# A dilation over 121 taps: chains of half-height relus in PSUM with one matmul for each step, twelve pairs added by DMA, and two pairs clamped by GpSimd

## The reference, cut to what matters

```python
v = _gn(x)
pad = jnp.pad(v, ..., constant_values=-1e30)          # 5 rows and columns on each side
for idx in range(121):
    di, dj = idx // 11, idx % 11
    acc = jnp.maximum(acc, pad[:, :, di:di+256, dj:dj+256] - kflat[:, idx])
x = x + acc
x = x + _L1_conv_ref(_gn(x), ...)                     # convolution, batch norm, gelu, bilinear resampling
```

## Time and profile before

| | |
|---|---|
| Time, median of 3 runs | 11728.51 us (11725.23 to 11729.66) |
| Span of the profiled execution | 11726.8 us |
| Dilation, first join to last join (63 chunks) | 367.3 to 9764.3 us |
| Convolution stage | about 9790 to 10700 us |
| Resampling stage | about 10720 us to the end |
| Busy share of the span | PE 89%, DVE 96%, ACT 78%, POOL 85% |

### The profile page before, as it was taken

The page is one execution under the profiler, slowest core; times in us unless marked ns, Lnnn a source line. Parts: engine busy times, 40 slices in busy tenths (PEclk is TensorE's granted clock), DMA queues, the critical chain, the costliest instruction groups (busy, mean ns, idle before and its releaser), DMA issues. The chain is left out here.

```text
span 11726.8 us, 92131 instructions
## 1 busy us (share of the span) xinstructions
PE 10455.5 (89%) x23180; PEld 4353.8 (37%) x23180; DVE 11256.4 (96%) x7096; ACT 9189.6 (78%) x5145; POOL 10018.7 (85%) x3019
## 2 busy tenths in 40 slices
PE   2999999999999999999999999999999997886665
PEld 1333333333333333333333333333333333332222
DVE  8999999999999999999999999999999998998999
ACT  2888888888888888888888888888888886776666
POOL 2999999999999999999999999999999996666777
PEclk9999999999999999999999999999999998998888
DMA  7555555555555555555555555555555553343555
GB/s 280 105 108 105 107 104 106 106 105 100 105 103 105 103 104 103 106 108 108 105 107 108 106 106 106 106 108 105 106 105 107 106 103 128 151 167 157 213 214 213
DMA packets 352237, 1435.57 MB, mean 122 GB/s; under 512 B 18896, under 2 KB 125520, under 8 KB 289616
## 3 DMA queue, kind: packets, MB, share of 16 engines
q0 software_dynamic: 183440, 762.23, 35.9%
q1 hardware_dynamic: 168256, 667.25, 15.3%
HBM read 465.90 MB, written 201.33 MB: 57 GB/s over the span
## 5 line engine op out<-in xcount | busy, mean ns | idle before, releaser
L502 POOL TENSOR_TENSOR m_pool<-r_pool,u 128x2048 f32<-128x2048 f32 x1792 | 7708.4, 4369 | 864.9 <-DVE acc_a L675 556.3
L531 PE MATMUL m_pe<-u,mats 128*128 128x512 f32 x10240 | 5375.2, 606 | 508.0 <-DVE acc_b L657 398.9
L533 PE MATMUL m_pe<-r_pe,mats 128*128 128x512 f32 x10240 | 5273.8, 596 | 0.0
L675 DVE SCALAR_TENSOR_TENSOR acc_a<-m_pool,kt,acc_a 128x2048 f32<-128x2048 f32 x1728 | 4059.9, 2349 | 54.5 <-POOL m_pool L502 41.0
L657 DVE SCALAR_TENSOR_TENSOR acc_b<-m_pe,kt,acc_b 128x1024 f32<-128x1024 f32 x2560 | 3246.0, 1278 | 103.2 <-PE m_pe L533 100.5
L531 PEld LDWEIGHTS m_pe<-u,mats 128*128 128x128 f32 x10240 | 1837.4, 191 | 3285.4 <-issue 1856.8
L533 PEld LDWEIGHTS m_pe<-r_pe,mats 128*128 128x128 f32 x10240 | 1948.4, 190 | 2510.3 <-issue 2510.3
L675 DVE SCALAR_TENSOR_TENSOR acc_a<-u,kt,acc_a 128x2048 f32<-128x2048 f32 x896 | 2103.8, 2348 | 4.5
L621 ACT ACTIVATE r_pool<-dx,gap_l 128x2048 f32<-128x2048 f32 x896 | 1778.6, 1993 | 329.7 <-POOL m_pool L502 326.2
L621 ACT ACTIVATE r_pe<-dx,gap_l 128x2048 f32<-128x2048 f32 x832 | 1659.1, 1994 | 364.2 <-PE m_pe L533 349.9
L592 ACT ACTIVATE t<-dx,gap_r 128x2048 f32<-128x2048 f32 x640 | 1284.7, 2007 | 10.4
(11 more groups left out here) (139 smaller groups left out, 5595.1 us busy)
## 6 DMA issues: line engine op xcount, KB each, us to landing
t<-dx POOLq DMA_DIRECT2D x640, 1059.0 KB, 8.4
u<-x_dram SPq DMA_DIRECT2D x28, 3328.0 KB, 28.7
xw<-x_scratch SPq DMA_DIRECT2D x64, 1152.0 KB, 6.9
hw<-h_scratch SPq DMA_DIRECT2D x66, 1024.0 KB, 8.9
x<-xc POOLq DMA_DIRECT2D x65, 1024.0 KB, 8.0
xt<-x_dram SPq DMA_DIRECT2D x32, 2048.0 KB, 14.4
xc<-x_dram SPq DMA_DIRECT2D x64, 1024.0 KB, 4.7
x_scratch<-x SPq DMA_DIRECT2D x64, 1024.0 KB, 9.6
```

Source lines behind the costliest of these rows:

```text
L502: nc.gpsimd.tensor_tensor(m_pool[slot(s, k, j, NPOOL)][:], r_pool[slot(s, k, j, NPOOL)][:], u[s][:, k * CR + di:k * CR + di + CR, base:bas ...
L531: nc.tensor.matmul(dst, ident, u[s][:, top:top + 2, base:base + W], start=True, stop=False)
L533: last = nc.tensor.matmul(dst, ident, r_pe[slot(s, k, j, NPE)][:, row:row + 2, :], start=False, stop=True)
L675: nc.vector.scalar_tensor_tensor(out=acc_a[:], in0=src, scalar=kt[:, col(di, base):col(di, base) + 1], in1=acc_a[:], op0=ALU.subtract, op1 ...
```

## The change

The 121 taps are divided anew. Per chunk:

- Six row sides become chains (`CHAINS`): in rows di 0 to 2 the columns 0 to 4, in rows 3 to 5 the columns 10 to 5. A chain is folded from the outside in, in PSUM, separately for the two halves of 4 rows (`chain[0]`, `chain[1]`, two banks each): ScalarE's relu (128x1024) reads the chain's banks and writes them back, TensorE adds the next slice of `dx` (with the identity or the negated identity) with one matmul for each bank and `start=False`, and in the last step adds `u`. A left chain has 4 steps, a right one 5: 27 steps, on 2 halves.
- 12 pairs have their relu written to one of three `t` buffers, `u` is added there by DMA (`add_u`), and VectorE reads `t`.
- 24 pairs go over GpSimd. 22 get ScalarE's relu as before. Two (`CLAMPED`) get none: GpSimd clamps a slice of `dx` with `tensor_scalar` into `m_pool` and then adds or subtracts it. `m_pool` has three buffers in place of two.
- 16 single taps, one of which starts `acc_b`.
- The order of each engine is a string of letters (a digit is a chain step or merge of that half; r relu for GpSimd, x relu for a DMA pair, b `start_b`, u sum, n normalise; m, y, s merges of `m_pool`, `t`, `u`; t add, c clamp, i DMA issue, d piece of `dx`, a `add_x`).

```diff
+CHAINS = ((0, "left"), (1, "left"), (2, "left"), (3, "right"), (4, "right"), (5, "right"))
+NPOOL, NDMA = 24, 12
+CLAMPED = (6, 18)
+ACT_ORDER = "x0r10r1x01r01bxr01r01u0rr10xn10r01u01xrn10r1r0nx10x1r01nr01r01xr01r01x01r01r01xr001x01x01r01r1r"
+PE_ORDER = "010101100101010100110101010101010101010101010010101101"
+DVE_ORDER = "smm10ssmmyssm0m1ymymssm0m1ysssmymym01msmmymys0m1ssymmmysm01ymym"
+POOL_ORDER = "ttiadtititdctttitdttitiditttittdicttittidittt"
...
-    NPOOL, NPE, NTRIPLE = 28, 20, 10
...
+    RP, MP, TP = 2, 3, 3
...
+    chain_steps = []
+    for ch, (di, side) in enumerate(CHAINS):
+        bases = range(1, 5) if side == "left" else range(9, 4, -1)
+        chain_steps += [(ch, step, base) for step, base in enumerate(bases)]
...
+                def add_u(c, s, k, j):
+                    di, base, outer = dma_pairs[j]
+                    pool.wait_ge(t_ready, c * NDMA + (j + 1))
+                    passed(pool, pool_turns)
...
+                def clamp(c, s, k, i):
...
+                    pool.wait_ge(a_done, a_free(c, "m", j, NPOOL, MP))
+                    passed(pool, pool_turns)
+                    nc.gpsimd.tensor_scalar(m_pool[j % MP][:], dx[s][:, k * CR + di:k * CR + di + CR, lo:lo + W],
+                                            floor, FAR if right else -FAR, first, second).then_inc(clamp_ready, 1)
+                def pair(c, s, k, j):
...
+                    pool.wait_ge(r_pool_ready, c * NRELU + (relu_no[j] + 1))
+                    pool.wait_ge(a_done, a_free(c, "m", j, NPOOL, MP))
+                    nc.gpsimd.tensor_tensor(m, r_pool[relu_no[j] % RP][:], rows, ALU.add).then_inc(m_pool_ready, 1)
...
-                                    for q in range(2):
-                                        row = (half * 2 + q) * 2
-                                        dst = m_pe[half][:, 2 * q:2 * q + 2, :]
-                                        top = k * CR + di + row
-                                        nc.tensor.matmul(dst, ident, u[s][:, top:top + 2, base:base + W],
-                                                         start=True, stop=False)
-                                        last = nc.tensor.matmul(dst, ident, r_pe[slot(s, k, j, NPE)][:, row:row + 2, :],
-                                                                start=False, stop=True)
...
+                def add_step(c, s, k, h, i):
...
+                    pe.wait_ge(chain_relu[h], c * NSTEP + (i + 1))
...
+                    for r in range(0, HR, 2):
+                        top = k * CR + di + h * HR + r
+                        added = nc.tensor.matmul(chain[h][:, r:r + 2, :], weight, src[:, top:top + 2, dj:dj + W],
+                                                 start=False, stop=True, skip_group_check=True)
+                    added.then_inc(chain_added[h], 1)
...
+                def chain_step(c, s, k, h, i):
...
+                    if step == 0:
...
+                        act.wait_ge(chain_taken[h], at(c, NCHAIN, ch))
+                    else:
+                        act.wait_ge(chain_added[h], c * NSTEP + i)
+                    gap = gap_r if right else gap_l
+                    nc.scalar.activation(chain[h][:], src, ACT.Relu, bias=gap[:, col(di, base):col(di, base) + 1],
+                                         scale=scale).then_inc(chain_relu[h], 1)
...
+                                elif kind == "r":
+                                    behind = relu_pairs[j - RP] - (NPOOL if j < RP else 0)
+                                    act.wait_ge(m_pool_ready, at(c, NPOOL, behind + 1))
...
+                                elif kind == "x":
+                                    act.wait_ge(a_done, a_free(c, "y", j, NDMA, TP))
+                                    pair_relu(s, k, dma_pairs[j], t[j % TP][:, :, 0:W]).then_inc(t_ready, 1)
...
+                def merge_chain(c, h, ch):
...
+                    dve.wait_ge(chain_added[h], c * NSTEP + (last_step[ch] + 1))
+                    dve.wait_ge(chain_taken[h], at(c, NCHAIN, ch))
+                    if ch == 0:
+                        dve.wait_ge(b_started, c + 1)
+                    nc.vector.scalar_tensor_tensor(out=part, in0=chain[h][:], scalar=kt[:, base:base + 1], in1=part,
+                                                   op0=ALU.subtract, op1=ALU.max).then_inc(chain_taken[h], 1)
...
+                    elif kind == "y":
+                        dve.wait_ge(t_added[j % TP], c * (NDMA // TP * 16) + (j // TP + 1) * 16)
```

More of the change, by code:

```diff
@@ L63, in passed @@
     engine.sem_inc(turns, 1)
[L66 to L82, removed]
-        singles += [(di, base), (di, outer)]
[L86 to L114, removed]
@@ new lines, in dilation_taps @@
+def dilation_taps():
+    pairs, singles = [], []
+    for di in range(KS):
+        side = dict(CHAINS).get(di)
+        if side == "left":
+            pairs += [(di, 5, 6), (di, 7, 8), (di, 9, 10)]
+        elif side == "right":
+            pairs += [(di, 1, 0), (di, 3, 2)]
+            singles += [(di, 4)]
+        else:
+            pairs += [(di, 5, 4), (di, 3, 2), (di, 6, 7), (di, 1, 0), (di, 8, 9)]
+            singles += [(di, 10)]
+    while len(pairs) > NPOOL + NDMA:
+        di, base, outer = pairs.pop()
+        singles += [(di, base), (di, outer)]
+    return pairs[NDMA:], pairs[:NDMA], singles
@@ L371, in dilation @@
         x1 = sb("x1", [P, CR, W])
-        t = [sb(f"t{s}", [P, CR * UC]) for s in range(2)]
+        neg_ident = sb("neg_ident", [P, P])
         acc_a = ctx.enter_context(nc.psum_tensor("acc_a", [P, CR, W], F32))
-        m_pe = [ctx.enter_context(nc.psum_tensor(f"m_pe{s}", [P, CR // 2, W], F32)) for s in range(2)]
+        chain = [ctx.enter_context(nc.psum_tensor(f"chain{h}", [P, HR, W], F32)) for h in range(2)]
         pads_set = sem("pads_set")
@@ L382, in dilation @@
         t_ready = sem("t_ready")
-        t_added = [sem(f"t_added{s}") for s in range(2)]
+        t_added = [sem(f"t_added{s}") for s in range(TP)]
         pool_turns = sem("pool_turns")
@@ L492, in _ @@
                             c = i * CH_IT + (s * CPW + k)
[L493 to L506, removed]
+                            for kind, j in numbered(POOL_ORDER):
+                                if kind == "t":
+                                    pair(c, s, k, j)
+                                elif kind == "c":
+                                    clamp(c, s, k, j)
+                                elif kind == "i":
+                                    add_u(c, s, k, j)
+                                elif kind == "a":
@@ L515, in _ @@
             @block.tensor
             def _(pe):
-                pe.sem_inc(m_pe_ready, NB)
+                pe.wait_ge(pads_set, 1)
+                for h in range(2):
+                    for r in range(0, HR, 2):
+                        opened = nc.tensor.matmul(chain[h][:, r:r + 2, :], ident, x1[:, r:r + 2, :],
+                                                  start=True, stop=True, skip_group_check=True)
+                    opened.then_inc(chain_open, 1)
+                def add_step(c, s, k, h, i):
+                    ch, step, base = chain_steps[i]
+                    di, side = CHAINS[ch]
+                    pe.wait_ge(chain_relu[h], c * NSTEP + (i + 1))
+                    if i == last_step[ch]:
+                        weight, src, dj = ident, u[s], base
+                    elif side == "left":
+                        weight, src, dj = neg_ident[:], dx[s], base
+                    else:
+                        weight, src, dj = ident, dx[s], base - 1
+                    for r in range(0, HR, 2):
+                        top = k * CR + di + h * HR + r
+                        added = nc.tensor.matmul(chain[h][:, r:r + 2, :], weight, src[:, top:top + 2, dj:dj + W],
+                                                 start=False, stop=True, skip_group_check=True)
+                    added.then_inc(chain_added[h], 1)
@@ new lines, in pair_relu @@
+                def pair_relu(s, k, pair, dst):
+                    di, base, outer = pair
+                    right = outer > base
+                    lo = base if right else outer
+                    gap = gap_r if right else gap_l
+                    return nc.scalar.activation(dst, dx[s][:, k * CR + di:k * CR + di + CR, lo:lo + W], ACT.Relu,
+                                                bias=gap[:, col(di, base):col(di, base) + 1],
+                                                scale=1.0 if right else -1.0)
@@ L629, in _ @@
+                for which in range(2):
+                    sum_before(NCHUNK, which, NWIN)
             @block.vector
@@ L636, in _ @@
                     nc.vector.memset(dx[s][:, :, UC - 1:UC], 0.0)
-                    nc.vector.memset(t[s][:].rearrange("p (r w) -> p r w", w=UC)[:, :, W:UC], 0.0)
+                for s in range(TP):
+                    nc.vector.memset(t[s][:, :, W:UC], 0.0)
+                nc.vector.tensor_scalar(neg_ident[:], ident, -1.0, None, ALU.mult)
```

254 lines of the change are left out of this document (120 added, 134 removed).

## The result

The changed kernel takes 11453.24 us (median of 4 runs, 11443.28 to 11457.96) against 11726.87 us before in runs beside it: ratio 0.9766, interval 0.9752 to 0.9780. It is faster by 2.3%, where 5.1% was forecast, and the time lies 53 us above the range. The profiled execution has a span of 11441.5 us.

The account below looks back on a forecast made before the run. VectorE was taken to bound the dilation: 137.6 us of work plus 2.0 of waits, 9.56 less a chunk, times 64 = 612; 11726.8 - 612 + 12 = 11127, as median 11129 us; range 10990 to 11400.

Parts of the forecast that it names:

- VectorE's floor: VectorE's own merges and join in a dilation chunk: 137.6 us, 8.6 less than the 146.2 before.
- ScalarE's and GpSimd's prices: Half relu in PSUM 1.10 us (1.01 after overlap); GpSimd clamp 4.1 us, bounds 1.8 and 8.3; both engines' sums covered by VectorE.
- clamps are dear: Rival: GpSimd's clamps at 8.3 us make VectorE wait some 4 us a chunk, 11385 us; chance 6%.
- TensorE, the step that failed: Chain step between ScalarE's relus: two matmuls together 1.02 us, 1.92 at low clock, fit the 2.8 us left nearly everywhere.
- a lower clock: TensorE's gaps of 1.5 to 5 us drop its clock in many places; only handovers to VectorE lose 0.9 us.
- the margins of 1 to 4 us at the merges: Second to fifth chains ready 1 to 4 us before VectorE asks for them; the low clock takes 0.9 of each.
- the normalisation: Four pieces on ScalarE, in the first chunk of a window only: 6.7 us of work.
- the chain becomes the bound: Rival: ScalarE and TensorE late at chain merges, 142 to 147 us a chunk, 11280 to 11600 us, 11440 for 144.5; chance 15%.
- The sum: Dilation chunk: VectorE's 137.6 us plus 2.0 of waits, 139.6 against 149.16 before.

Follow-up runs that it names:

- one bank: Add left out in the second bank, so one matmul for each chain step and half, against the changed kernel: 11203.87 us.
- the even order: Same instructions as the changed kernel, ScalarE's order new with spread chain steps and later normalisation, TensorE following: 11182.89 us, ratio 0.9538.
- the turn of the loop: ScalarE's loop over four windows in place of two, against the even order: 11140.83 us in one run.
- the even orders: The even order and a second new ScalarE order with short gaps between chain steps and the last relus for t spread out: 11182.89 and 11190.07 us.

## Why the prediction was wrong

**VectorE's floor, right.** 137.6 us of its own work; the second chunks with one bank show it bare, 137.75 us.

**ScalarE's and GpSimd's prices, right.** Half relu 1.09 for 1.10. Clamp 2.29 for 4.1, inside the bounds. The Trainium skill's GPSIMD Engine Reference (Engine selection) gives about line rate for one-input work, and the measurement agrees: 2.29 us beside VectorE's 2.35. GpSimd did not set the pace of the changed kernel (VectorE waited 41.0 us for it in the whole run). The rival "clamps are dear" is out, and the clamps carry the change: without them, in this order, it is no faster than before.

**TensorE, the step that failed.** "A relu of 1.10, the handover, two matmuls of 1.02 together ... A pair at 1.92 us still fits into 2.8." The row read as x2 was one float32 matmul in two records, not two matmuls. It was there to be seen in the kernel before: the group of L531 has 10240 records, 160 a chunk, where the code issues 80.

```profile
L531 PE MATMUL m_pe<-u,mats 128*128 128x512 f32 x10240 | 5375.2, 606 | 508.0 <-DVE acc_b L657 398.9
```

The add of a step takes 1.9 us at 2.4 GHz and 3.6 at 1.2. The first still fits into 2.8 us for one half; with both halves side by side ("01") the second half's add waits for the first's, and its way round, 1.09 + 1.7 + 1.9 = 4.7 us from the first relu's start on, has 0.2 us left of the 4.9 that the order gives. The trace of the changed kernel shows such a stretch at the higher level, the adds of both halves as eight records: TensorE works 3.71 of every 3.91 us.

```profile
3213.98 3.71 PE L525 MATMUL chain<-dx,mats 128*128 128x512 f32 x8 [0.24 <-ACT chain L588]
3217.89 3.70 PE L525 MATMUL chain<-dx,mats 128*128 128x512 f32 x8 [0.20 <-ACT chain L588]
```

At 3.6 us the add does not fit at all. So a delay is not made up for in such a stretch, and each gap of TensorE that brings the lower level, which the prediction priced at 0.9 us at a merge, pushes the following steps, until the margins of 1 to 4 us at the merges are used up. The experiment with one bank shows the size, 249 us; the even order shows that room between the steps gives back most of the waiting with all the work done.

The prediction reckoned with a lower clock, and the granted clock did fall, from 0.99 to 0.92; it took this for harmless because of the mis-sized pair. The Trainium skill (TensorE: Matmul & The Clock Gate, HAM oscillation) describes a kernel whose waits between bursts of matmuls throttle TensorE each time anew; this trace agrees, with an add at 0.51 behind a gap of 2.79 us.

**The window's load, missing.** Of the normalisation only the work was counted (6.7 us), not when its input lands. The new order puts the first piece some 12 us nearer to the join than the one before did (31.4 us for 43.9), and the load lands 4.4 us later than before. This is 112 us by experiment.

**The rival named "the chain becomes the bound" came true**, with the time it gave (11440) and for its place, at 15%. Its price for the half relu was not the reason, though; the reason was in TensorE's part. That its time is so near is luck: it was worked out from a relu at the upper price and waits for buffers, and neither is what held the chunks up.

**The sum.** Forecast 139.6 us a chunk, measured 144.6. Moving the normalisation takes 1.6 of the 5.0, the even steps 2.4 more, the turn of the loop 0.7. The three together, at 139.86 us, are about the forecast: 11141 measured, 11129 forecast. Nearly all of the missing gain was lost to order, not to work.

**Left open.** How much of the 249 us is the lower clock itself and how much the add at full clock: both shorten with one matmul less, and no run keeps the clock up otherwise. The trace of the changed kernel says how often it is low: of the 3398 adds between the first and the last join, 8% had a granted clock under 0.6 in the mean, another 9% one between 0.6 and 0.95. Why the turn of ScalarE's loop costs 5.2 us in the even order and under 1.9 in the changed kernel was not tried. Why the even orders stay 2 to 3 us above VectorE's floor is only known as many small waits, in the first of them 66.3 us for `start_b`, 55.7 for GpSimd's adds and 51.6 at the chain merges in the whole run.

## What to carry to other kernels

When two engines hand a buffer to and fro, add up one whole turn (both operations, at the clock that the gaps will leave) and hold it against the place that the order gives it; a sum of busy times says nothing about it. Check the count of a group against the count in the code before using its mean: if the count is twice that of the code, the operation is two records. For every item that moves in an order, ask what lands for it, and when; an engine that both issues DMAs and computes passes a wait ahead of an issue on to the work behind it; and where taking work off an engine changes nothing, change its order first.

## What was not expected of the hardware

- A float32 matmul of 128x512 is two records; two such matmuls took 1.88 us at 2.4 GHz and 3.58 at 1.2 GHz.
- ScalarE's relu in place in PSUM with a bias column takes 1.088 us for 1024 elements, while TensorE and VectorE use other banks; VectorE's merges kept 2.35 us beside it.
- GpSimd's `tensor_scalar` with two operations on 128x2048 took 1.96 us at least and 2.39 in the median, against 4.18 for the median add of two tensors.
- The turn of ScalarE's loop of four chunks took 5.0 to 5.4 us in the even order, and eight turns fewer gave 42 us (one run).
